# Slot loads issued behind chunk 1's sums, head 0's maxima placed before the last values, and the exp table fetched early

## What is computed

```python
def attn(x, ...):            # x: (2, 2048, 512), 16 heads of 32
    q, k, v = proj(Wq, bq), proj(Wk, bk), proj(Wv, bv)
    scores = einsum('bhqd,bhkd->bhqk', q, k) / sqrt(32)
    scores = scores + slopes[h] * distances[k]
    scores = where(causal, scores, finfo.min)
    ctx = einsum('bhqk,bhkd->bhqd', softmax(scores), v)
    return ctx @ Wo + bo

xn = layernorm(x)
out = x + attn(xn, ...) + experts(xn, ...)   # top 2 of 8, SiLU(gate) * up, down
```

## Time and profile before

| | |
|---|---|
| median of 3 executions | 2082.34 us (2071.69 to 2085.49) |
| profiled execution | 2078.22 us, span of its instructions 2076.2 us |
| busy in the span | PE 1954.8, ACT 1320.5, DVE 1442.9, POOL 1360.5 us |
| mean granted TensorE clock | 0.978 of full speed |
| bytes by DMA | 243.94 MB, mean 117 GB/s |

### The profile page before, as it was taken

The page is one execution under the profiler, slowest core; times in us unless marked ns, Lnnn a source line. Parts: engine busy times, 40 slices in busy tenths (PEclk is TensorE's granted clock), DMA queues, the critical chain, the costliest instruction groups (busy, mean ns, idle before and its releaser), DMA issues. The chain is left out here.

```text
span 2076.2 us, 38386 instructions
## 1 busy us (share of the span) xinstructions
PE 1954.8 (94%) x8670; PEld 1418.8 (68%) x8671; DVE 1442.9 (69%) x3391; ACT 1320.5 (64%) x2603; POOL 1360.5 (66%) x1199
## 2 busy tenths in 40 slices
PE   5999999899999999999999999999969989999996
PEld 4888877666767767676766667677637666666664
DVE  6445455788888888888888888898778833333332
ACT  3323321798998989899898989999852323333332
POOL 4110112788888889888888888888867535555554
PEclk9999999899999999999999999999989999999999
DMA  6667767442423233242423324232117755555554
GB/s 219 213 223 265 240 198 223 122 114 54 120 53 100 74 81 93 68 104 53 103 71 81 94 73 100 53 86 68 34 52 231 229 156 97 99 93 100 95 97 71
DMA packets 118487, 243.94 MB, mean 117 GB/s; under 512 B 15920, under 2 KB 52656, under 8 KB 112144
## 3 DMA queue, kind: packets, MB, share of 16 engines
q1 hardware_dynamic: 100464, 206.09, 34.3%
q0 software_dynamic: 17984, 37.38, 10.3%
HBM read 139.28 MB, written 104.21 MB: 117 GB/s over the span
## 5 line engine op out<-in xcount | busy, mean ns | idle before, releaser
L1061 POOL TENSOR_TENSOR probs_lo<-probs,probs_hi 128x512 fp32r<-128x512 f32 x800 | 1013.5, 1296 | 168.3 <-ACT probs L1092 168.0
L1091 ACT ACTIVATE probs_hi<-s_ps 128x512 fp32r<-128x512 f32 x928 | 597.4, 644 | 93.7 <-DVE s_ps L1155 91.2
L1092 ACT ACTIVATE probs<-s_ps 128x512 f32<-128x512 f32 x960 | 595.5, 651 | 0.2 <-DVE s_ps L1155 0.2
L1134 DVE TENSOR_REDUCE m_part<-m_ps 128x1 f32<-128x512 f32 x744 | 490.7, 684 | 11.3 <-PE m_ps L1369 5.6
L1385 PE MATMUL s_ps<-q_st,k_st 100*128 100x512 f32 (+3 forms) x880 | 323.6, 409 | 35.2 <-ACT probs L1092 17.1
L1369 PE MATMUL m_ps<-k_st,q_st 98*128 98x512 f32 (+2 forms) x840 | 281.7, 377 | 0.0
L1403 PE MATMUL o_ps<-probs_hi,v_split 128*96 128x512 f32 (+3 forms) x748 | 279.0, 383 | 1.0 <-POOL probs_lo L1061 0.5
L1404 PE MATMUL o_ps<-probs_lo,v_split 128*96 128x512 f32 (+3 forms) x748 | 269.9, 364 | 0.0
L1131 DVE CUSTOM_DVE_ANT_0 m_ps<-m_ps,mask_row 128x128 f32<-128x128 f32 x496 | 241.6, 497 | 19.2 <-PE m_ps L1369 12.8
L1385 PEld LDWEIGHTS s_ps<-q_st,k_st 100*128 100x128 f32 x880 | 159.2, 190 | 128.4 <-ACT probs L1092 55.4
L1759 POOL DMA_INDIRECT out<-y,tile_rows x71 | 114.2, 1609 | 170.9 <-issue 99.8
(11 more groups left out here) (202 smaller groups left out, 3615.9 us busy)
## 6 DMA issues: line engine op xcount, KB each, us to landing
v_d<-v_rows SPq DMA_DIRECT2D x7, 3072.0 KB, 9.4
v_split<-v_d SPq DMA_DIRECT2D x22, 768.0 KB, 8.4
k_st<-k_hi_d SPq DMA_DIRECT2D x44, 256.0 KB
q_st<-q_hi_d SPq DMA_DIRECT2D x44, 256.0 KB
xs<-in_x SPq DMA_DIRECT2D x8, 1024.0 KB, 6.8
xn_d<-xs SPq DMA_DIRECT2D x8, 1024.0 KB, 11.4
q_hi_d<-qk_hi SPq DMA_DIRECT2D x32, 256.0 KB, 7.6
q_lo_d<-qk_lo SPq DMA_DIRECT2D x32, 256.0 KB, 7.9
```

The costliest lines, as they stand in the source:

```text
L1061: nc.gpsimd.tensor_tensor(*low_operands(u), ALU.subtract).then_inc(lo_ready_pool, 1)
L1091: nc.scalar.activation(probs_hi[:, P_SLOT[u]], scores, ACT.Exp, scale=SCALE)
L1092: nc.scalar.activation(scores if KIND[u] == "Q" else probs[:, P_SLOT[u]], scores, ACT.Exp, scale=SCALE).then_inc(p_ready, 1)
L1134: V.tensor_reduce(top, scores, AX.X, ALU.max).then_inc(m_taken, 1)
```

## The change

Four parts.

1. In `attend`, SP issues the loads of slot n + 2 (and gate_up in the heads that have it) after the store of chunk 1's sums in head n, and no longer at the head's beginning. `load_values` of head 1 moves along in head 0.
2. Head 0's maxima begin with the k tiles of chunk 6, one beside each. These first four use the bank `mp` alone (`FIRST_ALONE`), since `xt` still holds x. Chunk 7's values tiles 1 to 3 have none beside them any more.
3. The fold is made after the first values tile of chunk 7, PE's transpose before the third, the rows before the fourth is kept, and SP places the rows ahead of both halves of the last values store.
4. ACT runs one exponential of a 128x1 column at the end of stage 1, so that the table for exp is loaded there.

```diff
-    beside = ((0,) * 2 * G + (3, 3, 3, 2), (0, 3, 3, 3, 2) + (3,) * 6 + (0,))
+    beside = ((0,) * G + (1,) * G + (3,) * TPC, (1, 3, 3, 3, 2, 3, 3, 3, 3, 0, 0, 0))
+    FIRST_ALONE = sum(beside[0][:2 * G])
...
-            return (mp, xt[:, 0], xt[:, 1])[m % FIRST_BANKS]
+            return mp if m < FIRST_ALONE else (xt[:, 0], xt[:, 1], mp)[(m - FIRST_ALONE) % FIRST_BANKS]
...
+                if last:
+                    sp.wait_ge(q_ones, 1)
+                    sp.wait_ge(m_rows_ready, 1)
+                    for dst, src in maxima_places(t, 0):
+                        sp.dma_start(dst, src).then_inc(m_placed, 16)
                 step = TPC // 2 if last else TPC
...
+            nc.scalar.activation(sd[:, 0:1], sd[:, 0:1], ACT.Exp)
...
                 for j in range(TPC):
                     beside(2 * G + j)
+                    if last and j == 1:
+                        fold_maxima()
+                    if last and j == TPC - 1:
+                        maxima_rows()
                     keep_values(c, j)
...
-                if m >= FIRST_BANKS:
-                    pe.wait_ge(m_taken, m - FIRST_BANKS + 1)
+                if FIRST_ALONE <= m < FIRST_ALONE + 2:
+                    pe.wait_ge(xl_ready, 2 + KD * NCH)
                 elif m:
-                    pe.wait_ge(xl_ready, 2 + KD * NCH)
+                    pe.wait_ge(m_taken, m if m < FIRST_ALONE else m - FIRST_BANKS + 1)
...
+                    if last and j == 2:
+                        pe.wait_ge(m_taken, M_SLOTS)
+                        nc.tensor.transpose(mp[0:QT, 0:P], m_max[:, :], ident).then_inc(m_scored, 1)
...
                 sums = 0
-                if load_ahead:
-                    if before:
-                        sp.wait_ge(pv_done, PV_START + NS * n)
-                    load(n + 2, (r + 2) % HEADS_RING)
                 for kind, u, back in ATTEND:
                     if kind == "O" and (before or not back):
                         store_context(n - back, u)
...
+                    if kind == "O" and u == 1 and load_ahead:
+                        if before:
+                            sp.wait_ge(pv_done, PV_START + NS * n)
+                        else:
+                            load_values(n + 1, r + 1)
+                        load(n + 2, (r + 2) % HEADS_RING)
+                        if gate_up is not None:
+                            load_gate_up(gate_up)
```

More of the change, by code:

```diff
@@ L383, in first_bank @@
         def first_bank(m):
-            return (mp, xt[:, 0], xt[:, 1])[m % FIRST_BANKS]
+            assert FIRST_ALONE == 4
+            return mp if m < FIRST_ALONE else (xt[:, 0], xt[:, 1], mp)[(m - FIRST_ALONE) % FIRST_BANKS]
         small_loaded = sem(ctx, "small_loaded")
@@ L506, in _ @@
             chunk(NCH - 1, 1, False, last=True)
[L507 to L510, removed]
             sp.wait_ge(small_loaded, 16 * N_SMALL)
@@ L743, in take_maximum, with fold_maxima @@
                     nc.vector.tensor_reduce(top, scores, AX.X, ALU.max).then_inc(m_taken, 1)
-            def maxima_rows():
+            def fold_maxima():
                 dve.wait_ge(m_taken, NM)
@@ L748, in maxima_rows @@
                                         ).then_inc(m_taken, 1)
+            def maxima_rows():
                 dve.wait_ge(m_scored, NM + 1)
@@ L763, in chunk @@
                         x_low(c + 1, 1 - par, g - G)
-                    if g:
-                        beside(g)
+                    beside(g)
                     qk_low(c, g)
@@ L792, in _ @@
             chunk(NCH - 1, 1, False, last=True, first_maxima=FIRST_MAXIMA[1])
-            maxima_rows()
         @block.tensor
@@ L879, in _ @@
             chunk(NCH - 1, 1, False, last=True, first_maxima=FIRST_MAXIMA[1])
-            pe.wait_ge(m_taken, M_SLOTS)
-            nc.tensor.transpose(mp[0:QT, 0:P], m_max[:, :], ident).then_inc(m_scored, 1)
 def attend(nc, sb, ps, sem, t):
@@ L986, in _, with step_n @@
             load_values(0, 0)
-            load_values(1, 1)
             sp.wait_ge(k_ones, HEADS_RING)
             sp.wait_ge(q_ones, HEADS_RING)
-            def step_n(n, r, load_ahead=True, maxima=True, before=True, after_sums=0, then=None):
+            def step_n(n, r, load_ahead=True, maxima=True, before=True, after_sums=0, then=None, gate_up=None):
                 sums = 0
-                if load_ahead:
-                    if before:
-                        sp.wait_ge(pv_done, PV_START + NS * n)
-                    load(n + 2, (r + 2) % HEADS_RING)
                 for kind, u, back in ATTEND:
@@ L1038, in _ @@
                 for k in range(1, HEADS_RING + 1):
-                    step_n(HEADS_RING * i + k, k % HEADS_RING)
-                    if k == 1:
-                        load_gate_up(i)
+                    step_n(HEADS_RING * i + k, k % HEADS_RING, gate_up=i if k == 1 else None)
             for n in range(HEADS_RING * E + 1, NH - 1):
```

## The result

| | before | after |
|---|---|---|
| median of 8 runs, us | 2077.59 (2071.69 to 2085.49) | 2092.11 (2087.99 to 2099.58) |
| profiled execution, us (span) | 2078.22 (2076.2) | 2087.99 (2086.2) |
| mean granted clock | 0.978 | 0.970 |

The ratio is 1.007, with an interval of 1.0051 to 1.0089. I had forecast 2068 and a range of 2053 to 2082, so the median went 14.5 us up instead of 14 down.

What follows compares the result with a forecast made beforehand. PE, busy 94% of the span, was taken to bound the kernel; -23.0 + 1 + 12 + 0.8 - 3.8 - 1 = -14 us against the profiled 2078.2 gave 2064.2, hence 2068 for the median, range 2053 to 2082.

Steps and rivals of the forecast that it cites:

- head 0: In head 0, v_split of head 1 stands ahead of the slot and delays the next maxima: 0.8 us lost, 0 to 1.5.
- the boundary: Between projection and first scores: scores 4.8 us earlier, one us given back at the first values, net -3.8, bounds -2 and -6.
- the projection with the early maxima: First four maxima moved into chunk 6's projection are no more work for PE: 0 to -2 us, -1 taken.
- with the semaphore 1.5, eight times = 12 us: In eight heads with gate_up ahead of the maxima, PE waits 1.5 us each: 12 us lost, bounds 6 to 18.
- I count the 23.0 us in full: In the heads, ACT's wait for the late sums store goes and periods shorten one for one: 23.0 us gained.
- Rival (b): In the heads, removing ACT's wait gives only PE's own 12.4 us: 2079 us; chance 0.16.
- In 22 of 30 heads they just miss the tail: In heads without gate_up, the placed maxima wait 0 to 0.4 us each behind the slot's bytes; 1 us in all.
- rival (c): In all 30 heads the slot drains in 13 us or more and the maxima are late: slower, 2110 us; chance 0.07.
- Rival (a): In the eight gate_up heads the maxima are not held by gate_up: 12 us less, 2056 us; chance 0.22.
- 4.8 us earlier: At the boundary, first scores start at 365.1 instead of 369.90, as maxima and rows are done beside the values tiles.
- Two of them come before a PE stall of 2.82 us ... so they fit in it: In chunk 6's projection, two early maxima and any wait for slot 0 at 283 fit in an existing stall.
- Zero either way: At the end of stage 1, moving the 1.28 us exp table load ahead neither gains nor costs time.

Runs made afterwards that it cites:

- e1: The changed kernel with the two gate_up loads back at the head's end: 2064.14 us, ratio 0.9928 to before.
- e10: The changed kernel with seven matmuls that nothing reads ahead of PE's wait for the placed maxima, in ten of 32 heads: 2087.32 us, ratio 1.0027 to before.
- e7: The changed kernel with both gate_up DMAs issued by POOL on its own queue at the fold: 2093.63 us, ratio 1.0067 to before.
- e9: The changed kernel with gate_up at the head's end, first maxima two tiles later, head 0's loads at its beginning: 2063.01 us, ratio 0.9937 to before.
- e2: The changed kernel with the first stage of before, slot loads and gate_up still moved: 2093.06 us, ratio 1.0065 to before.
- e11: The kernel before with only the slot loads of heads 1 to 29 moved behind chunk 1's store, head 0's left early: 2064.84 us, ratio 0.9916 to before.
- e3: The kernel before with parts 2 to 4 of the change alone and no load moved: 2082.09 us, ratio 1.0017 to before.
- e5: The kernel before with only the slot loads, and v_split of head 1, moved behind chunk 1's store: 2066.33 us, ratio 0.9929 to before.
- e6: The changed kernel with only gate_up's gate half (512 KB) behind the slot, the up half at the head's end: 2072.79 us, ratio 0.9965 to before.

## Why the prediction was wrong

Between the two profiled executions the span grew by 10.0 us: 3.9 up to the first T, 11.2 in the heads, and 5.0 less in the code behind them that is the same. The sum had -4.8 and -9.2 for the first two. Term by term, forecast and measured: slot loads -22 and -18.7, gate_up +12 and +27.8, head 0 +0.8 and +2.1, the boundary -3.8 and -0.8, the projection with the early maxima -1 and +4.7, the code behind 0 and -5.0. The heads' 11.2 are -18.7 for 29 periods without gate_up's share (e1 against before), +2.1 for head 0 (38.63 against 36.54) and +27.8 for gate_up (the changed kernel against e1).

**The step that failed is "with the semaphore 1.5, eight times = 12 us".** The wait itself was sized right: 1.5 us forecast, 1.48 to 1.86 measured, 13.4 in all. What it does to PE's clock was left out. I priced a new idle stretch of PE at its own length and gave it bounds of 6 to 18 us, where it cost 27.8. e10 shows the missing half: with PE at work through the same wait, the heads give 12.8 us back. The rows to see it by stood ahead of the prediction. The 7.87 us of idle time at the boundary had a window at 0.86 around it, and I used that in the sentence on the boundary alone. In windows of 1 us before has 13.7 us at half clock from 363 on, and 3.4 us from 291 on, by the stall of 2.82 us; behind PE's waits of up to 1.0 us there are none. A wait of 1.5 us lay between, and its bounds had to hold both: 1.5 alone, and 1.5 with 3.4 us at half clock, which is 1.7 us of work lost, an estimate of 3.2 us a head and 26 in all. With 26 for 12 the sum is 0 and the forecast 2082, still some 10 us short; most of these are in the boundary and the projection below.

**The slot loads' term: right in kind, 3 us too large.** "I count the 23.0 us in full", with 1 given back, made -22; measured -18.7 in the 29 periods behind the first, in which ACT had waited 22.2 of the 23.0 us. The periods are now 35.48 and, in the first head of an iteration, 35.86. The second isn't new: laid against ACT's waits head by head, the periods of before less the wait are 35.3 to 35.5, and 35.7 in the first head of each iteration. So 0.1 us a head didn't come back, 3.5 in all; my floor of 35.42 from one head was too low for the mean. In each head PE still waits 0.45 to 0.5 us for an exponential at T + 3.4: the row `PE s_ps L1396 <- ACT probs L1103: 13.7, 29, 0.5`. Rival (b), at most the 12.4 us that PE itself lost, fell: the periods gave 18.7. But that PE's idle time explains the gain isn't shown. From 410 to 1500 us PE's waits for exponentials fell by 9.6 us only (24.2 to 14.6 in e1), those of its weight loads by 25.9 (75.1 to 49.2), and no run says how the 18.7 us divide between them.

**What drains when.** "In 22 of 30 heads they just miss the tail" held better than said: in the changed kernel no plain head waits for its maxima (in e10's trace one does, 0.95 us). That falls rival (c) too, in which all heads had such a wait; its side was right and its mechanism wrong. Rival (a), no wait at all, fell by the eight waits. That the order in the ring holds the maxima back was the text's reason; e7 shows that gate_up on another queue holds them back as long.

**Head 0: 0.8 forecast, 2.1 measured** against before, and 3.1 against e9, whose head 0 has no such wait (38.63 and 35.56). The reason is the same: a wait of 1.3 us and 3.4 us at half clock behind it, at 410.

**The boundary: "4.8 us earlier".** Up to the first scores it was right, counted from the projection's end: 9.1 us before, 369.50 - 364.41 = 5.1 less the last matmuls' 1.07, so 4.0 after. But of these 5.1 us only 0.8 are left at the first T, which comes 39.8 us behind the projection's end before and 39.0 after (38.8 to 39.6 in all traces with the changed first stage, 39.8 to 40.0 in those with the old). The windows from the first scores to the first T, before and changed:

```profile
369.90:400.60 30.70, 30.70 (x130) 22.69 (x131) 28.46 (x70) 26.92 (x55) 25.17 (x20) 0.89 0.49 131
```

```profile
369.50:404.40 34.90, 32.51 (x129) 23.96 (x129) 28.58 (x70) 27.22 (x55) 25.25 (x20) 0.81 0.51 154
```

The half-clock stretch is 13.7 us in both, but it lasts from 363.2 to 376.8 before and from 369.0 to 382.7 after. So 7.0 us of it came behind the first scores before and 13.2 after: half of the 6.2 more, 3.1 us, is lost. The wait of 2.39 us for `v_split`, for which one us had been given back, lies in that stretch too and so costs only half, 1.2 us: 5.1 - 3.1 - 1.2 = 0.8. I had expected a shorter stretch behind a shorter idle time, and it came later instead.

The bound from before the end of the projection was wrong too: that end came 4.7 us later. "Two of them come before a PE stall of 2.82 us ... so they fit in it" failed by one tile: the first maximum stands one tile ahead of the place that I took for it, PE reaches it at 279.4 and not at 283, and slot 0 has landed only at 284. The two stalls of PE in the last two chunks, 2.82 and 0.90 us in before, are 4.59 and 0.89 here, 1.8 us more. Even that isn't sure: e2 and e11, with the first stage of before, have 3.2 and 3.3 us where before has 2.82, and e3, with the changed one, waits 3.00 and ends its projection at the same 365.5. The other 3 us or so are the clock. In the window from 300 to 330 the granted clock is 0.98 before and 0.89 after, but 0.89 and 0.94 in e5 and e11 too, whose first stage is that of before:

```profile
300.00:330.00 30.00, 30.00 (x163) 25.76 (x162) 17.31 (x51) 5.28 (x8) 8.69 (x6) 0.98 0.62 185
```

```profile
300.00:330.00 30.00, 30.00 (x137) 25.26 (x136) 17.79 (x53) 4.60 (x7) 6.54 (x5) 0.89 0.56 175
```

The first is the kernel before, the second the changed one. The projection ends at 360.8, 363.8, 364.0 and 368.2 us in the four traces with the first stage of before, and at 365.4 to 371.4 with the changed one. With the first stage of before the first T came at 400.6, 403.6, 403.8 and 408.2, with the changed one at 404.3 to 410.3. The profiled execution of before had the earliest of them all, and no first T shows a gain; nor do the runs' ratios, 1.0065 and 1.0070 for e2 and the changed kernel, 0.9929 and 0.9928 for e5 and e1, 1.0017 for e3. What stays open is whether the early maxima cost these 3 us or whether single executions differ by them.

**"Zero either way" for the table load** held. It runs at 366.89, ACT is at work again at 368.18, and the barrier is passed near 369. The Trainium skill (ScalarE: Activation LUTs, "What ACT_TABLE_LOAD costs") has a drain of some 1.4 us on top of the load's 1.28; here the ACTIVATE stands 1.29 us behind the load's start, and the load itself 0.02 us behind the end of the one ahead of it, so no such drain shows.

## What to carry to other kernels

When a large load is moved so that it ends next to a small DMA which the busiest engine waits for, count the bytes that the 16 engines still have to move at that moment, on all queues: half a megabyte less made eight waits of 1.7 us into nearly none, and moving it to another queue changed nothing. Price a new wait of TensorE by the waits of like length that the trace has, with the granted clock of the stretch behind them, and not by its length alone. Let what two changes share be moved one at a time: the slot loads alone gave 0.7%, and the two loads that moved along with them took 1.4%.

## What was not expected of the hardware

- Eight waits of 1.48 to 1.86 us on an otherwise full TensorE came with 27.2 us at 1.2 GHz, in pieces of 3.4 or 6.8 us, at five of them; which ones didn't go by the length (1.48 us had 6.8, 1.71 none). e2 has the same five pieces, e7 six, 30.7 us together. Waits of up to 0.6 us (e6's four) had none. Of the five of 0.84 to 0.98 us for maxima in e5, e6, e7 and e10, three had 3.4 us, all in the head behind the boundary.
- Seven matmuls whose output nobody reads, in the place of the wait, kept the clock at 1.00 and made the kernel 9 us faster by the runs' ratios.
- Two DMAs of 8 KB landed 3.5 us after issue behind 1 MB on their own queue and 3.8 us with the same 1 MB on another and the slot's end ahead on their own, against 1.8 us with idle rings.
